# One kernel, four edits: values of the 16 context rows computed in front, u of two chunks in the stage before, 16-bit rounding and a rebuilt loop in the 8-bit feed forward, one block moved in the time mixing

## The chip, the core and the metric

The kernel runs on one core of a Trainium2 chip. The core has TensorE (PE; its weight loads, PEld, are shown apart), VectorE (DVE), ScalarE (ACT), GpSimd (POOL) and SyncE (SP, which here issues DMAs). The metric is the time of one execution on the device in microseconds, the median of several runs.

## The reference, cut to what matters

Four layers of three sublayers each work on x of 32 batches, 64 tokens and 256 features, and on a context of 32 x 128 rows of 128 features. Each sublayer computes `x = x + f(layernorm(x))`. These are the ones that the change touches.

The narrow cross attention (layers 1 to 3) splits the 128 context rows of a batch: the last 16 ("dca") have keys and values from weights of their own.

```python
kv_dca = (y_dca @ Wkv_dca + bkv_dca).reshape(b, DCA, 2, H, HD)
k_dca = _ln(kv_dca[:, :, 0], kn_dca_w, kn_dca_b);  v_dca = kv_dca[:, :, 1]
q = _ln((x @ Wq + bq).reshape(b, s1, H, HD), qn_w, qn_b)
...
ctx = _attn(qT, k, v) + DCA_WEIGHT * _attn(qT, k_dca, v_dca)   # two softmaxes
return ctx @ Wo + bo
```

The feed forward of layer 2 rounds the operands of its products to 8-bit floats and keeps results in bf16:

```python
def _qdot(x, w, out_dtype=BF16):
    return jnp.dot(x.astype(E4M3), w.astype(E4M3), preferred_element_type=out_dtype)
gate_value = jax.nn.gelu(_qdot(x, w_gating[0]))
activations = gate_value * _qdot(x, w_gating[1])
return _qdot(activations, w_linear)
```

The state space layer of layer 3 runs `h = exp(delta * A) * h + delta * B_t * xc` over the 64 tokens for 512 channels and 16 states, and sums `h * C_t` over the states. The product `delta * xc` is called u. The time mixing of layer 2 is a WKV recurrence with exponents, and a sigmoid gate r.

## The kernel before, in words

The twelve sublayers are blocks that follow one another (`SUBLAYERS`, L3680). In a block each engine has its own list of instructions, in the order in which the code issues them; counters (`sem[...]`) tell one engine what another has done, and nothing else sets the order. Activations lie transposed: features on the 128 partitions, the 2048 tokens as columns in four chunks of 512 (`CH`).

**Narrow cross attention (function from L1380).** In front of the loop the norm, the merged weights and the first three units of queries and keys are made. `widen(2)` (L1563) is the last of these, with a `keep_warm` (L79) on each side; `keep_warm` multiplies ones into a bank that nobody reads. Then come 36 steps. In step n TensorE makes the scores of batch n+1 (L1576) in the four banks `p_s`, the values of batch n-2 (L1587), the mixture of batch n-3 (L1615), turns the probabilities of batch n-2 (L1602), and every second step makes an output product (L1622). The units left over are spread over the steps: products (L1537, L1541), variance (L1553), widening (L1563). The values product has 512 columns: the first 256 by the main weights, the last 256 by the dca weights, of which only 16 rows are used. ScalarE copies both parts into `vx` (L1741, and L1743 for the 16 rows). VectorE takes the maxima of the scores (L1803), subtracts (L1813), sums (L1821), inverts (L1824), multiplies a unit (L1797) and adds the output (L1829). GpSimd scales the probabilities (L1889).

**Time mixing.** ScalarE's list begins with the norm, keys and values of chunk 0, then `gate(0)` (a load of the sigmoid table, two sigmoids L2736, a load of the exponential table) and then `exponents(0, 0)` and `exponents(0, 1)` (L2750, L2756).

**8-bit feed forward (`gated_fp8`).** 16 pairs of hidden tiles, each 2 x 128 features by 512 tokens. For a pair TensorE makes gate and up of two tiles (L2979, eight products) and adds the pair before the last but one to the output (`down`, L2993, four products; `LAG` is 2). ScalarE copies gate and up to bf16 (L3035, L3036), takes the gelu (L3038), and unloads an output chunk (L3019). VectorE's `round_pair` multiplies (L3064), cuts out the exponent (L3066), makes from it a large number (L3071), and adds and subtracts it (L3073, L3077), which rounds to 8-bit precision. The sum between the two, `moved`, is an f32 tile. VectorE also rounds the inputs in chunks (`move_h`, L3049 to L3057), scales the norm of the last two chunks and adds the residual (L3081). ScalarE's inverse of that norm (L3026 to L3029) lies behind the fourth pair.

**State space (`state_space`).** A first block makes `xc`, `delta` and the rows of B and C. The main block goes over 8 chunks of 256 columns and 16 states. ScalarE makes decay factors (L3540), GpSimd or TensorE the driving term, VectorE scans (L3607, L3609), GpSimd or VectorE weighs, TensorE sums (L3487). For the states 1, 4, 7, 10 and 14 the driving term comes from TensorE (L3471) by a turned copy of u (L3461, copied at L3524) and diagonals of B (L3517). GpSimd makes u of a chunk in `begin` (L3557) and marks batch starts (L3561): of chunk 0 at the block's start, of the next chunk at state 7. TensorE begins with eight warming products, two turns, and four warming products.

## Time and profile before

| | us |
|---|---|
| three runs | 2979.25, 2980.6, 2981.99 (median 2980.6) |
| profiled execution, device time | 2980.97 |
| its span | 2979.2 |
| TensorE busy | 2686.3 (90%) |
| VectorE busy | 1851.0 (62%) |
| ScalarE busy | 1409.8 (47%) |
| GpSimd busy | 1041.1 (35%) |
| mean granted TensorE clock | 0.971 of full speed |

The shares are averages over stages with different limits, so they are to be read stage by stage. By the first and last instruction of each, the narrow attentions run from 850.4 to 1058.0, from 1499.4 to 1708.7 and from 1945.5 to 2153.2; the time mixing from 1708.7 to 1844.5, the 8-bit feed forward to 1945.5, the state space layer's first block from 2153.2 to 2277.3 and its main block to 2685.7. An f32 product of TensorE stands in the trace as two records. A granted clock of 1.0 is 2.4 GHz and 0.5 is 1.2 GHz.

### The profile page before, as it was taken

How to read it: one execution, taken by the hardware profiler on the slowest of the kernel's cores; microseconds unless marked ns; L12 is line 12 of the kernel's file. 1: busy time of each engine (PE TensorE's matmuls, PEld its weight loads, DVE VectorE, ACT ScalarE, POOL GpSimd, SP SyncE). 2: the span in 40 equal slices, each digit the busy share in tenths (PEclk: the TensorE clock that was granted, in tenths of full speed). 3: DMA queues.
4: the chain of work that ended last, by engine and by line, in shares of the span. 5: the costliest groups of instructions: out<-in, count | busy, mean ns of one | idle time of the engine just before them, and what ended most of it. 6: DMA issues, size and time to landing. Idle time of an engine off the chain costs nothing. (4 is left out here: it accounts for less than half of the span.)

```text
span 2979.2 us, 51028 instructions
## 1 busy us (share of the span) xinstructions
PE 2686.3 (90%) x19340; PEld 1704.2 (57%) x19344; DVE 1851.0 (62%) x2513; ACT 1409.8 (47%) x2684; POOL 1041.1 (35%) x885
## 2 busy tenths in 40 slices
PE   7999997999989998899989977689997889997998
PEld 5999963466656647533346623246643555554787
DVE  3666646322248827543558788968755999996332
ACT  3323335121147747432247775657676666652223
POOL 1222210133216614100026500035502999981562
PEclk9999999999999999999999988899999999999999
DMA  4000002311120000110000000000001111103224
GB/s 162 22 25 25 18 7 99 134 47 46 54 62 2 2 23 3 42 47 0 1 24 2 16 1 1 0 24 2 27 19 50 71 73 71 73 36 123 70 82 147
DMA packets 77017, 128.95 MB, mean 43 GB/s; under 512 B 12112, under 2 KB 54736, under 8 KB 76304
## 3 DMA queue, kind: packets, MB, share of 16 engines
q1 hardware_dynamic: 67888, 101.78, 10.2%
q0 software_dynamic: 8928, 24.39, 2.6%
q8 instruction: 138, 2.26, 0.3%
q14 instruction: 63, 0.52, 0.1%
HBM read 107.40 MB, written 18.74 MB: 42 GB/s over the span
## 5 line engine op out<-in xcount | busy, mean ns | idle before, releaser
L3577 POOL TENSOR_TENSOR h<-ssm_u,ss_bc 128x1024 f32<-128x1024 f32 x88 | 205.6, 2357 | 0.0
L3540 ACT ACTIVATE ssm_p_h<-ss_delta,ss_decay 128x256 f32<-128x256 f32 x352 | 146.5, 464 | 123.9 <-DVE ctxT L3614 81.7
L3487 PE MATMUL ssm_p_y<-ctxT,ident 128*128 128x512 f32 x412 | 187.7, 596 | 0.0
L684 POOL TENSOR_TENSOR xw_prob<-xw_prob,xw_rsum 128x512 f32<-128x512 f32 x64 | 65.2, 1040 | 259.2 <-DVE xw_rsum L633 259.2
L3609 DVE TENSOR_TENSOR_SCAN ssm_p_h<-ssm_p_h,h 128x1024 f32<-128x1024 f32 x64 | 145.8, 2279 | 8.9 <-ACT ssm_p_h L3540 6.8
L3567 POOL TENSOR_TENSOR ctxT<-ctxT,ss_bc 128x1024 f32<-128x1024 f32 x50 | 117.4, 2356 | 19.8 <-DVE ctxT L3607 19.8
L3487 PEld LDWEIGHTS ssm_p_y<-ctxT,ident 128*128 128x128 f32 x412 | 76.5, 192 | 79.2 <-issue 78.5
L515 PE MATMUL xw_p_q<-h,xw_m_h 128*128 (+1 forms) x1024 | 119.0, 277 | 1.3 <-PEq L61 1.3
L515 PEld LDWEIGHTS xw_p_q<-h,xw_m_h 128*128 128x128 f32 x1024 | 116.0, 192 | 7.0 <-issue 7.0
L3471 PE MATMUL ssm_p_h<-ssm_b_diagonal,ssm_uT 128*128 128x128 f32 x640 | 82.0, 282 | 41.7 <-DVE ctxT L3614 21.2
L523 PE MATMUL xw_p_q<-xw_u,xw_vo_h 128*128 128x128 f32 x1024 | 117.1, 275 | 1.2 <-ACT xw_u L587 1.2
L617 DVE TENSOR_TENSOR xw_prob<-xw_p_s,xw_mask_bias 128x512 f32<-128x512 f32 x64 | 43.5, 680 | 119.0 <-PE xw_p_s L534 112.0
L523 PEld LDWEIGHTS xw_p_q<-xw_u,xw_vo_h 128*128 128x128 f32 x1024 | 115.6, 192 | 1.6 <-ACT xw_u L587 1.6
L3471 PEld LDWEIGHTS ssm_p_h<-ssm_b_diagonal,ssm_uT 128*128 128x128 f32 x640 | 77.0, 195 | 65.5 <-issue 56.7
L2524 ACT ACTIVATE lmm_hidden<-lmm_p_h,vecs 128x512 f32<-128x512 f32 x64 | 43.8, 687 | 135.8 <-PE lmm_p_h L2462 120.2
L1232 DVE TENSOR_TENSOR L0f_hidden<-L0f_silu,L0b_p_u 128x512 f32<-128x512 f32 x39 | 26.8, 688 | 125.4 <-PE L0b_p_u L1167 109.6
L582 ACT ACTIVATE xw_prob<-xw_prob 128x512 f32<-128x512 f32 x64 | 38.9, 633 | 111.2 <-DVE xw_prob L624 111.2
L1141 POOL DMA_INDIRECT L0f_rows_out<-L0b_y,L0f_row_of x39 | 38.5, 986 | 146.7 <-DVE L0b_y L1240 146.7
L1889 POOL TENSOR_TENSOR L1x_prob<-L1x_prob,L1x_rsum 128x896 f32<-128x896 f32 x64 | 65.3, 1042 | 64.6 <-DVE L1x_rsum L1824 64.6
L1889 POOL TENSOR_TENSOR L3x_prob<-L3x_prob,L3x_rsum 128x896 f32<-128x896 f32 x64 | 65.3, 1042 | 64.3 <-DVE L3x_rsum L1824 64.3
L1889 POOL TENSOR_TENSOR L2x_prob<-L2x_prob,L2x_rsum 128x896 f32<-128x896 f32 x64 | 65.3, 1042 | 64.2 <-DVE L2x_rsum L1824 64.2
L1861 POOL MEMSET L2x_vx<- 128x1024 f32 x1 | 1.0, 956 | 244.7 <-POOLq L61 244.7
(872 smaller groups left out, 7104.6 us busy)
## 6 DMA issues: line engine op xcount, KB each, us to landing
ss_bc<-ss_bc_rows SPq DMA_DIRECT2D x24, 896.0 KB, 4.3
xw_ctx_rows<-in_ctx_rows SPq DMA_DIRECT2D x32, 256.0 KB, 2.6
ss_bc<-ss_bc_rows SPq DMA_DIRECT2D x8, 768.0 KB, 4.0
L3f_rows<-L3f_rows_out SPq DMA_DIRECT2D x16, 384.0 KB, 3.9
L0f_wg<-in_L_ffn_gate SPq DMA_DIRECT2D x9, 512.0 KB, 9.4
L0f_wu<-in_L_ffn_up SPq DMA_DIRECT2D x9, 512.0 KB, 9.5
L0f_wd<-in_L_ffn_down SPq DMA_DIRECT2D x9, 512.0 KB, 9.6
L0f_rows<-L0f_rows_out SPq DMA_DIRECT2D x16, 256.0 KB, 4.3
```

What stands on the lines that cost most here:

```text
L515: mm = pe.matmul(p_q5[:, q % 2, h % 4 // 2, :, h % 2, :], m_h[:, h, a, :], k.h[:, a, ts(i, P)], start=h % 4 == 0 and a == 0, stop=a == H2 ...
L523: mm = pe.matmul(p_q[:, 1, ts(o, P)], vo_h[:, h, ts(o, P)], us[:, h, :], start=h == 0 and o == 0, stop=h == NH - 1, skip_group_check=True)
L617: v.tensor_tensor(prob[:, b, part, :], p_s[:, part, :], bcast(bias[:, ts(n, S2)], 1, 4), ALU.add).then_inc(sem["masked_scores"], 1)
L684: g.tensor_tensor(prob[:, n % 2, part, :], prob[:, n % 2, part, :], bcast(rsum[:, 1, part], 2, S2), ALU.mult).then_inc(sem["normed"], 1)
L1889: scaled = g.tensor_tensor(prob[:, m % 4, :, :, s0:s1], prob[:, m % 4, :, :, s0:s1], bcast(rsum[:, 1, m % 4, seg, :, :], 3, s1 - s0), ALU. ...
L2524: act.activation(hh[:, slot, j, :], p_h[:, slot, :], ACT.Gelu_apprx_tanh, bias=bias1[:, m:m + 1]).then_inc(sem["gelued"], 1)
L3471: mm = pe.matmul(p_h[:, n % 2, e * CT + b * P:e * CT + b * P + P], uT[:, c % 2, b, ts(e, P)], db[:, i, b, :], start=True, stop=True, skip_ ...
L3487: mm = pe.matmul(p_y[:, 2 * half:2 * half + 2, :].rearrange("p e t -> p (e t)"), k.ident[:, :], weighed[n % RING_W][:, ts(half, CH)], star ...
L3540: i = act.activation(out[:, ts(e, CT)], delta[:, e, ts(c, CT)], ACT.Exp, scale=decay[:, E4 * s + e:E4 * s + e + 1])
L3567: g.tensor_tensor(tiles(weighed[n % RING_W]), tiles(weighed[n % RING_W]), bcast(bcs[:, row_c(s), :], 1, E4), ALU.mult).then_inc(sem["weigh ...
L3577: g.tensor_tensor(tiles(drive[n % RING]), u[:, c % 2, :, :], bcast(bcs[:, row_b(s), :], 1, E4), ALU.mult).then_inc(sem["driven_g"], 1)
L3609: v.tensor_tensor_scan(slot, factor, term, 0.0, ALU.mult, ALU.add).then_inc(sem["scanned"], 1)
```

## The change

**Attention.** The 16 dca rows of all batches are gathered at the start by GpSimd into the tile of `us`. After `widen(2)`, in place of the second `keep_warm`, TensorE makes the values of eight batches at a time in four products of 256 columns, in the banks `p_s` that the first scores need next. ScalarE copies them out in two copies, SP moves the 16 rows of each batch to partitions 0 to 15 with 32 DMAs, and ScalarE's second copy of a batch reads that tile. The values product in the loop has 256 columns. **Time mixing.** `gate(0)` stands behind `exponents(0, 0)`. **Feed forward.** `moved` is bf16, with a smaller large number. ScalarE copies gate and up of a tile in one instruction and takes the gelu of a pair in one; the inverse of the norm is behind the first copies; `LAG` is 3; the output tile has two buffers; VectorE's extra work is spread differently. **State space.** GpSimd makes u of chunks 0 and 1, and marks their starts, in the first block. The warming goes down to one product between the two turns; ScalarE makes diagonals one state at a time.

```diff
+            for n in range(B):
+                g, j = n // GROUP, n % GROUP
+                if j == 0:
+                    sp.wait_ge(sem["dca_copied"], g // 2 + 1)
+                    if g >= 2:
+                        sp.wait_ge(sem["v_copied"], GROUP * (g - 1))
+                sp.dma_start(dca_values[:, n % (2 * GROUP), :], dca_made[DCA * j:DCA * j + DCA, g, :]).then_inc(s_d[g], 16)
...
                     pe.wait_ge(sem["scaled"], EARLY)
+                    pe.wait_ge(sem["dca_copied"], B // GROUP // 2)
...
+            def values_of_dca():
+                pe.wait_ge(s_o, 32)
+                pe.wait_ge(sem["dca_gathered"], 1)
+                pe.wait_ge(sem["scaled"], 2)
+                for g in range(B // GROUP):
+                    mm = pe.matmul(p_sf[:, g // 2, ts(g % 2, D)], dca_keys[:, ts(g, P)], wv[:, 1, :], start=True, stop=True, skip_group_check=True)
+                    if g % 2 == 1:
+                        mm.then_inc(sem["dca_made"], 1)
...
-                pe.matmul(p_v[:, :], k.ctxT[:, ts(n, S2)], wv[:, :, :].rearrange("p n f -> p (n f)"), start=True, stop=True, skip_group_check=True).then_inc(sem["valued"], 1)
+                pe.matmul(p_v[:, 0:D], k.ctxT[:, ts(n, S2)], wv[:, 0, :], start=True, stop=True, skip_group_check=True).then_inc(sem["valued"], 1)
...
             widen(2)
-            keep_warm(pe, k, p_tw[:, 0, :], 1)
+            values_of_dca()
...
-                    act.copy(own(m, slice(0, DCA)), p_v[0:DCA, D:2 * D].rearrange("p (g j d) -> p g j d", j=2, d=HD)).then_inc(sem["v_copied"], 1)
+                    if m % GROUP == 0:
+                        act.wait_ge(s_d[m // GROUP], 16 * GROUP)
+                    act.copy(own(m, slice(0, DCA)), dca_values[:, m % (2 * GROUP), :].rearrange("p (g j d) -> p g j d", j=2, d=HD)).then_inc(sem["v_copied"], 1)
...
+            for n in range(B // GROUP // 2):
+                act.wait_ge(sem["dca_made"], n + 1)
+                act.copy(dca_made[:, 2 * n:2 * n + 2, :].rearrange("p g f -> p (g f)"), p_sf[:, n, :]).then_inc(sem["dca_copied"], 1)
...
+            g.tensor_copy(dca_keys.rearrange("p (b s) -> p b s", s=DCA), k.ctxT[:, :].rearrange("p (b s) -> p b s", s=S2)[:, :, 0:DCA]).then_inc(sem["dca_gathered"], 1)
...
             keep(0, 1)
-            gate(0)
+
...
             exponents(0, 0)
+            gate(0)
             exponents(0, 1)
...
-    NP, LAG = PAIRS * NCH, 2
+    NP, LAG = PAIRS * NCH, 3
...
-        gb = sb(k, ctx, "gate", [P, 2, CH], BF16)
-        ub = sb(k, ctx, "up", [P, 2, 2, CH], BF16)
+        gu = sb(k, ctx, "gate_up", [P, 2, 2, 2, CH], BF16)
...
-        mv = sb(k, ctx, "moved", [P, 2, CH])
+        mv = sb(k, ctx, "moved", [P, 2, CH], BF16)
         aq = sb(k, ctx, "act", [P, LAG + 1, 2, CH], BF16)
-        yb = sb(k, ctx, "out", [P, H2, CH], BF16)
+        yb = sb(k, ctx, "out", [P, 2, H2, CH], BF16)
...
-                    pe.wait_ge(sem["copied"], 2 * (m - 1))
+                    pe.wait_ge(sem["copied"], m - 1)
...
-                if 1 <= n < 3:
-                    ln.var(pe, n - 1)
                 if n >= LAG:
                     down(n - LAG)
                 if n < NP:
                     project(2 * n + 1)
+                if n == 0:
+                    ln.var(pe, 0)
+                    ln.var(pe, 1)
...
-            act.preload_act_table(ACT.Gelu_apprx_tanh)
...
-                if c >= 1:
-                    act.wait_ge(sem["residual"], c)
-                act.copy(yb[:, :, :], outs[c % 2][:, :, :]).then_inc(sem["unloaded"], 1)
+                if c >= 2:
+                    act.wait_ge(sem["residual"], c - 1)
+                act.copy(yb[:, c % 2, :, :], outs[c % 2][:, :, :]).then_inc(sem["unloaded"], 1)
+
+            for n in range(NP):
+                if n > LAG + 1 and (n - LAG - 2) % PAIRS == PAIRS - 1:
                     unload((n - LAG - 2) // PAIRS)
-                if m == 8:
-                    act.preload_act_table_set("natural_log_exp_and_others")
+                if n >= 2:
+                    act.wait_ge(sem["product"], n - 1)
+                for j in range(2):
+                    act.wait_ge(sem["proj"], 2 * n + j + 1)
+                    act.copy(gu[:, n % 2, j, :, :], p_g[:, j, :, :]).then_inc(sem["copied"], 1)
+                if n == 0:
                     ln.inverse(act, 0)
                     ln.inverse(act, 1)
                     act.preload_act_table(ACT.Gelu_apprx_tanh)
-                act.wait_ge(sem["proj"], m + 1)
-                if n >= 2:
-                    act.wait_ge(sem["product"], n - 1)
-                if m >= 2:
-                    act.wait_ge(sem["gelued"], m - 1)
-                act.copy(gb[:, m % 2, :], p_g[:, m % 2, 0, :]).then_inc(sem["copied"], 1)
-                act.copy(ub[:, n % 2, m % 2, :], p_g[:, m % 2, 1, :]).then_inc(sem["copied"], 1)
-                act.wait_ge(sem["copied"], 2 * m + 1)
-                act.activation(ge[:, n % 2, m % 2, :], gb[:, m % 2, :], ACT.Gelu_apprx_tanh).then_inc(sem["gelued"], 1)
-            unload(NCH - 1)
+                act.wait_ge(sem["copied"], 2 * n + 2)
+                act.activation(ge[:, n % 2, :, :], gu[:, n % 2, :, 0, :], ACT.Gelu_apprx_tanh).then_inc(sem["gelued"], 1)
+            for c in range((NP - LAG - 2) // PAIRS, NCH):
+                unload(c)
...
-                v.tensor_scalar(mg[:, :, :], ex[:, :, :], FP8_MIN_NORMAL, FP8_MAGIC, ALU.max, ALU.mult).then_inc(sem["magic"], 1)
+                v.tensor_scalar(mg[:, :, :], ex[:, :, :], FP8_MIN_NORMAL, FP8_MAGIC16, ALU.max, ALU.mult).then_inc(sem["magic"], 1)
                 v.wait_ge(sem["magic"], n + 1)
                 v.tensor_tensor(mv[:, :, :], ac[:, :, :], mg[:, :, :], ALU.add).then_inc(sem["moved"], 1)
...
-                if n == 4:
-                    ln.scale(v, 0)
-                    ln.scale(v, 1)
-                elif n in (5, 6):
-                    move_h(n - 3)
+                if n in (3, 7):
+                    ln.scale(v, n // 4)
+                elif n in (4, 8):
+                    move_h(n // 4 + 1)
...
+                g.wait_ge(sem["delta"], 1)
+                g.wait_ge(sem["xc"], E4)
+                for c in range(MADE):
+                    make_input(g, c).then_inc(sem["input"], 1)
+                g.wait_ge(sem["input"], MADE)
+                for c in range(MADE):
+                    mark_starts(g, c)
...
-            keep_warm(pe, k, p_t[:, :], 8)
             turn(0, 0)
+            keep_warm(pe, k, p_o[:, :, :].rearrange("p o t -> p (o t)"), 1)
             turn(0, 1)
-            keep_warm(pe, k, p_o[:, :, :].rearrange("p o t -> p (o t)"), 4)
             driven(1)
...
-            for i in range(NT_):
-                for b in range(2):
-                    diagonal(0, i, b)
+            for b in range(2):
+                diagonal(0, 0, b)
             for n in range(TOTAL):
                 c, s = n // N, n % N
-                act.wait_ge(sem["starts"], c + 1)
+                if c >= MADE:
+                    act.wait_ge(sem["starts"], c + 1 - MADE)
...
-                if n < 2:
-                    turned(0, n)
+                if n == 0:
+                    turned(0, 0)
+                    turned(0, 1)
+                if 1 <= n < NT_:
+                    for b in range(2):
+                        diagonal(0, n, b)
...
-                if c >= 2:
-                    g.wait_ge(sem["turned"], 2 * (c - 1))
-                g.tensor_tensor(u[:, c % 2, :, :], delta[:, :, ts(c, CT)], xc[:, :, ts(c, CT)], ALU.mult).then_inc(sem["input"], 1)
-                g.wait_ge(sem["input"], c + 1)
-
-                first = delta[:, :, ts(c, CT)].rearrange("p e (b t) -> p e b t", t=S)[:, :, :, 0:1]
-                g.tensor_scalar(first, first, 0.0, 1e28, ALU.mult, ALU.add).then_inc(sem["starts"], 1)
+                g.wait_ge(sem["turned"], 2 * (c - 1))
+                make_input(g, c).then_inc(sem["input"], 1)
+                g.wait_ge(sem["input"], c + 1 - MADE)
+                mark_starts(g, c).then_inc(sem["starts"], 1)
...
-            begin(0)
```

TensorE in front of the third attention's loop, before (`L3x_p_t`: the warming's bank, `L3x_p_s`: the scores' banks, `L3x_rv`: inverse deviations):

```order
L1553 MATMUL L3x_p_y<-L3x_square,L3x_tally 32x128 x8
L79 MATMUL L3x_p_t<-ones 128x512
L1563 MATMUL L3x_p_s<-L3x_rv,L3x_heads 128x128 x8
L79 MATMUL L3x_p_t<-ones 128x512
L1576 MATMUL L3x_p_s<-L3x_k,L3x_qx 128x128 x8
```

and now (`L3x_u` holds the gathered dca rows, `L3x_wv` the value weights):

```order
L1566 MATMUL L3x_p_y<-L3x_square,L3x_tally 32x128 x8
L80 MATMUL L3x_p_t<-ones 128x512
L1576 MATMUL L3x_p_s<-L3x_rv,L3x_heads 128x128 x8
L1599 MATMUL L3x_p_s<-L3x_wv,L3x_u 128x256 x4
L1590 MATMUL L3x_p_s<-L3x_k,L3x_qx 128x128 x8
```

The warming product between widening and scores has become four products into the banks that the scores take next.

ScalarE in the feed forward, from the table load to the first gelus, before:

```order
L3011 ACT_TABLE_LOAD
L208 ACTIVATE f_ln_square<-h 128x1024 x2
L3014 ACT_TABLE_LOAD
L3035 CAST f_gate<-f_p_g 128x512
L3036 CAST f_up<-f_p_g 128x512
L3038 ACTIVATE f_gelu<-f_gate 128x512
```

and now (`f_gate_up` holds both halves of a pair):

```order
L3041 ACT_TABLE_LOAD
L209 ACTIVATE f_ln_square<-h 128x1024 x2
L3057 CAST f_gate_up<-f_p_g 128x1024 x2
L215 ACTIVATE f_ln_rstd<-f_ln,eps 128x512
L217 ACTIVATE f_ln_rstd<-f_ln_rstd 128x512
L215 ACTIVATE f_ln_rstd<-f_ln,eps 128x512
L217 ACTIVATE f_ln_rstd<-f_ln_rstd 128x512
L3061 ACT_TABLE_LOAD
L3063 ACTIVATE f_gelu<-f_gate_up 128x1024
L3057 CAST f_gate_up<-f_p_g 128x1024 x2
```

The inverse of the norm (L214, L216, now L215, L217) has moved from behind the fourth pair to ahead of the first gelu, and one table load has gone from the start.

TensorE at the start of the state space layer's main block, before (`ssm_p_t`: turned u, `ssm_b_diagonal`: diagonals of B):

```order
L79 MATMUL ssm_p_t<-ones 128x512 x8
L3461 MATMUL ssm_p_t<-ident,ssm_u 128x128 x8
L79 MATMUL ssm_p_o<-ones 128x512 x4
L3471 MATMUL ssm_p_h<-ssm_b_diagonal,ssm_uT 128x128 x16
L3481 MATMUL ssm_p_y<-ss_xc,ss_diag 128x256 x4
```

and now:

```order
L3503 MATMUL ssm_p_t<-ident,ss_u 128x128 x4
L80 MATMUL ssm_p_o<-ones 128x512
L3503 MATMUL ssm_p_t<-ident,ss_u 128x128 x4
L3513 MATMUL ssm_p_h<-ssm_b_diagonal,ssm_uT 128x128 x16
L3523 MATMUL ssm_p_y<-ss_xc,ss_diag 128x256 x4
```

The turns stand first, and of twelve warming products one is left, between them.

## Rows read from the trace of the kernel before

**Rows 1.** busy time by stage; columns as in its first line
```profile
core 0: us, PE busy (x) PEld busy (x) DVE busy (x) ACT busy (x) POOL busy (x), PEclk, DMA share, GB/s
...
1844.50:1945.50 101.00, 66.67 (x208) 25.10 (x212) 87.39 (x104) 63.22 (x110) 0.00 (x0) 0.81 0.00 1
1945.50:2153.20 207.70, 192.13 (x2548) 125.64 (x2548) 159.34 (x266) 139.65 (x288) 108.14 (x119) 0.99 0.03 10
...
2277.30:2685.70 408.40, 363.01 (x1432) 217.62 (x1433) 374.83 (x208) 244.65 (x610) 372.70 (x169) 0.99 0.17 61
```

**Rows 2.** timeline of TensorE, one batch of the third narrow attention
```profile
2090.06 0.73 PE L1576 MATMUL L3x_p_s<-L3x_k,L3x_qx 32*128 32x128 f32 x16
2090.71 1.12 PE L1587 MATMUL L3x_p_v<-L3x_wv,ctxT 128*128 128x512 f32 x2
2093.38 0.65 PE L1553 MATMUL L3x_p_v<-L3x_square,L3x_tally 128*32 128x128 f32 x16
```

**Rows 3.** groups by line: the values product, and one of 256 columns
```profile
L1587 PE MATMUL L3x_p_v<-L3x_wv,ctxT 128*128 128x512 f32 x64 | 35.3, 633 | 0.0
L3452 PE MATMUL ssm_p_o<-ss_z,ss_w_out 128*128 128x256 f32 x128 | 29.0, 380 | 1.3 <-DVE ss_z L3588 1.3
```

**Rows 4.** waits of VectorE in that attention's loop (1979 to 2140)
```profile
DVE L3x_nmax L1803 <- PE L3x_p_s L1576: 10.2, 14, 2.7
DVE x L1829 <- PE L3x_p_y L1622: 6.2, 7, 2.5
```

**Rows 5.** timeline of VectorE, two batches near the loop's end
```profile
2124.53 1.28 DVE L1803 TENSOR_REDUCE L3x_nmax<-L3x_p_s 128x8 f32<-128x896 f32 x2
2132.73 1.27 DVE L1803 TENSOR_REDUCE L3x_nmax<-L3x_p_s 128x8 f32<-128x896 f32 x2
```

**Rows 6.** timeline in front of the loop: warming and first scores
```profile
1977.48 1.13 PE L79 MATMUL L3x_p_t<-ones 128*128 128x512 f32 x2
1978.97 0.73 PE L1576 MATMUL L3x_p_s<-L3x_k,L3x_qx 32*128 32x128 f32 x16 [0.36 <-DVE L3x_k L1797]
```

**Rows 7.** groups by line in the 8-bit feed forward
```profile
L3064 DVE TENSOR_TENSOR f_product<-f_gelu,f_up 128x1024 bf16<-128x1024 bf16 x16 | 11.0, 687 | 7.7 <-ACT f_gelu L3038 7.5
L3071 DVE TENSOR_SCALAR f_magic<-f_exponent 128x1024 bf16<-128x1024 bf16 x16 | 6.8, 427 | 0.6
L3073 DVE TENSOR_TENSOR f_moved<-f_product,f_magic 128x1024 f32<-128x1024 bf16 x16 | 19.6, 1226 | 0.6
L3019 ACT CAST f_out<-f_p_y 128x1024 bf16<-128x1024 f32 x2 | 2.0, 1012 | 0.0
```

**Rows 8.** timeline there: ScalarE's table loads, VectorE's products
```profile
1852.28 1.28 ACT L3014 ACT_TABLE_LOAD   x1
1853.57 0.58 ACT L3035 CAST f_gate<-f_p_g 128x512 bf16<-128x512 f32 x1
1856.69 0.69 DVE L3064 TENSOR_TENSOR f_product<-f_gelu,f_up 128x1024 bf16<-128x1024 bf16 x1 [1.68 <-ACT f_gelu L3038]
1877.82 0.69 DVE L3064 TENSOR_TENSOR f_product<-f_gelu,f_up 128x1024 bf16<-128x1024 bf16 x1 [3.58 <-ACT f_gelu L3038]
```

**Rows 9.** timeline of ScalarE, first sigmoid block of the time mixing
```profile
1736.61 0.60 ACT L2736 ACTIVATE tm_gate<-tm_p_p 128x512 f32<-128x512 f32 x1 [0.94 <-PE tm_p_p L2648]
```

**Rows 10.** timeline, start of the state space main loop
```profile
2277.36 9.24 PE L79 MATMUL ssm_p_t<-ones 128*128 128x512 f32 x16 [7.74 <-PEq L61]
2291.70 1.95 PE L3471 MATMUL ssm_p_h<-ssm_b_diagonal,ssm_uT 128*128 128x128 f32 x16
2293.75 2.29 DVE L3607 TENSOR_TENSOR_SCAN ctxT<-h,ssm_p_h 128x1024 f32<-128x1024 f32 x1 [6.96 <-PE ssm_p_h L3471]
2298.37 3.43 PE L3471 MATMUL ssm_p_h<-ssm_b_diagonal,ssm_uT 128*128 128x128 f32 x16 [4.72 <-DVE ctxT L3607]
```

**Rows 11.** timeline there, GpSimd's second u and a wait behind it
```profile
2307.69 2.36 POOL L3557 TENSOR_TENSOR ssm_u<-ss_delta,ss_xc 128x1024 f32<-128x1024 f32 x1
2322.04 2.30 DVE L3609 TENSOR_TENSOR_SCAN ssm_p_h<-ssm_p_h,h 128x1024 f32<-128x1024 f32 x1 [0.93 <-POOL h L3577]
```

36 lines of the change are left out of this document (23 added, 13 removed).

## The prediction

> **What bounds the kernel now.** I read the busy time by stage first, because one core runs twelve sublayers behind one another and the change touches six of them: three narrow cross attentions, the time mixing, the 8-bit feed forward and the state space layer. In each I then read who waits, and last the timeline at the edited place. The reader is to see three different bounds. In the cross attention (207.7 us, the other two within 2 us of it) TensorE is busy for 192.1 us and VectorE for 159.3 [rows 1], and VectorE's waits in the loop over batches are for scores and output products of TensorE [rows 4]. In the feed forward VectorE is busy for 87.4 of 101.0 us, and in the main loop of the state space layer for 374.8 of 408.4, with GpSimd at 372.7 [rows 1]. So TensorE's time counts in the attentions, VectorE's in the feed forward, and in the state space layer what delays the first scans.
>
> **Attention, loop: -7.5 us a layer.** The values product of a batch goes from 512 to 256 columns. It is two records per product, 64 in a layer [rows 3], 1.12 us of TensorE with no idle time around them [rows 2]. A record of 512 columns lasts 592 ns where nothing delays it and one of 256 lasts 380 on average [rows 3], so a record loses 0.213 us, a batch 0.427 and the layer 13.6. That is the most that it can give, and VectorE's waits in the loop, 10.2 and 6.2 us [rows 4], leave room for it. It is not all got: VectorE waits for scores 14 times in 32 batches, and each wait gives back at most what TensorE has saved since the one before, and never more than its own length. Where VectorE does not wait, the batch is set by its own work: maximum, subtraction, sum and reciprocal, 4.1 us (two batches from 2124.53 to 2132.73 [rows 5]), against 3.3 of TensorE from a batch's scores to the next part in one without a projection (2090.06 to 2093.38 [rows 2]). The last eight batches and some in the middle are such. That leaves 16 to 20 batches of 0.427: 6.8 to 8.5, and I take 7.5. Bounds: 4 (every second wait is replaced by one for GpSimd or ScalarE) and 11. The second copy per batch stays on ScalarE, now from the SBUF tile; ScalarE has idle time of its own before these copies, so its source costs nothing that shows. The 32 DMAs of 16 KB wait on SP only for the copies and are wanted over 15 us later.
>
> **Attention, front: +1.2 us a layer.** A warming product (two records, 1.13 us) goes; four products of 256 columns, eight records, come, and two copies of 512 columns on ScalarE. Before, the last widening is issued by 1977.48, where the warming begins, and the scores start at 1978.97, released by VectorE's multiplication [rows 6]. Now the records take 8 x 0.227 = 1.8 us (29.0 us for 128 records [rows 3]), the first copy lies beside the second half, and the second copy (about 0.6, half of the 1.01 of a copy of 1024 [rows 7]) stands behind the last record with two hand-overs of some 0.15: 1980.2. The multiplication is hidden now, the copy is what is late. Bounds 0.5 and 2.5. The gather on GpSimd stands at the stage's start, where it has nothing else to do. Three layers: 3 x (-7.5 + 1.2) = -19.
>
> **Time mixing: -1 us.** ScalarE's first sigmoid block waits 0.94 us for TensorE in its middle [rows 9]; now the first exponents stand ahead of it and the product is there when it is reached. Both table loads stay. What is queued behind is the same. Bounds 0 and -3.
>
> **Feed forward: -19 us.** Per pair VectorE does 0.687 + 2 x 0.427 + 2 x 1.226 us [rows 7]; the exponent's operation (L3066) is as long as that of L3071, the subtraction (L3077) as long as the addition. The two last write or read an f32 tile; with that tile 16 bit wide they have the types of the product row, 0.687. So 1.08 us a pair, 16 pairs, -17.2. Then the waits: VectorE waits 7.7 us for gelus [rows 7], 3.58 of it behind ScalarE's block of two table loads and four activations [rows 8]. The block moves ahead of the first gelu and one pair of loads is gone. ScalarE: two copies (0.9 each as issued one behind the other) from 1852.3, the four activations 2.6, a load 1.28, a gelu of 1024 about 1.0 (as the copy of 1024): the first product starts at 1859.1 and not 1856.7, +2.4. The other waits (0.9 + 0.2 + 3.6 + 1.2) go, -5.9. ScalarE then needs 2 x 0.9 + 1.0 = 2.8 us a pair, VectorE 2.9, plus 0.9 a pair for h, the norm and the residual. TensorE's twelve records a pair are 2.6 us at the full clock and 5.2 at half, and the granted clock of the stage is 0.81 [rows 1]. It has an idle stretch of some 3 us behind its first two pairs, as before, and I expect the next records at 1.2 GHz while VectorE has nothing in reserve: +1.7. Sum -17.2 - 5.9 + 2.4 + 1.7 = -19. What is late next is ScalarE in the pairs without other work on VectorE. Bounds: -10 (half clock in half of the pairs) and -22.
> What the Trainium skill adds here (ScalarE: Activation LUTs, "What ACT_TABLE_LOAD costs") is that a switch of tables costs a drain of about 1.4 us beside the 1.28. The trace disagrees: the load at 1852.28 lasts 1.28 and the work behind it starts at 1853.57 [rows 8]. By the page's rule the stage would gain 1.4 more.
>
> **State space: -9 us.** Before, TensorE warms for 9.24 us ahead of the two turns of u and 3.6 behind them, so that the products of state 1 start at 2291.7 and VectorE's second scan at 2293.75 after 6.96 us of idle [rows 10]. Now u is there when the block opens at 2277.3: first turn beside ScalarE's table load (1.28), two diagonals 0.6, decay factors 1.7 (2280.8), copy 0.6, second turn 1.1, copy 0.6, so 2283.2. The products take 1.95 us, or 3.43 as the next ones do at half clock [rows 10]; with the warming gone I take 3.4. Second scan at 2286.7: -7. GpSimd's 2.36 us of u for the second chunk at 2307.7 go from the first chunk too; VectorE's two waits on GpSimd behind it, 0.93 and about 1.2, go: -2 [rows 11]. The rest of the layer is VectorE and GpSimd in step and shifts as it is. In the stage before, GpSimd does both chunks of u with nothing else to do. Bounds -5 (further products at half clock) and -12.
>
> **Sum.** -19 - 1 - 19 - 9 = -48 us on a profiled span of 2979.2; that execution took 2980.97, 0.4 above the median 2980.6. The prediction is 2933 us.
>
> **Rivals.**
> A. VectorE takes over in the attentions. For it: in the tail of the loop it is the bound already, and its busy time is 159 us of 208. Against: TensorE is at 192, and 16 us of waits on it are real [rows 4]. Then the loop gives 2 a layer and the front costs 1.2: total -48 + 16.5 = -31, 2949 us.
> B. The feed forward changes its bound to TensorE. For it: twelve records at half clock (5.2 us) are longer than the new VectorE pair. Against: with a shorter pair TensorE rests less than it did in the pairs that ran at full clock. Price: half of 16 pairs at 5.2 in place of 3.8, +9 to +11: 2943 us.
> C. The 16-bit add and subtract run at the f32 rate, so that this part does not do what it says. The product row with the same three types speaks against it. Then the feed forward gains waits alone, -2: 2950 us.
> D. Slower than before: TensorE doesn't come up to 2.4 GHz in the state space layer. Its full-clock records there were preceded by sixteen dense warming records; now there are two, and turns. In a chunk TensorE works about 46 of 51 us at full clock; at half it would need some 35 more. It decides the sign from one and a half chunks on: with two at 1.2 GHz the time is 2933 + 70 = 3003 us. Against: at 2298 half clock was granted and left again within the next few groups, while the work was the same as now.
> What the Trainium skill says (TensorE: Matmul & The Clock Gate, on the transpose mode) is that transposes don't count as activity; by it the turns in front do not help to raise the clock. No row here separates turns from other work. It would favour D, or the half clock that I have assumed for the first products.
> E. More than forecast: all waits fall together with less half clock (loop 11 a layer, feed forward -22, state space -12): 2917 us.
>
> **How the numbers follow.** Forecast 0.62, A 0.14, B 0.10, C 0.03, D 0.02, E 0.09. The range reaches from near E to A's time: 2919 to 2949. About 0.2% (6 us) is what a measurement of this kernel can tell from no change. All cases but D are more than 29 us faster; for unseen couplings between the four edits I leave a little more: faster 0.95, same 0.02, slower 0.03.
>
> **What would show it.** In the profile after: values records near 380 ns with 13 us less of TensorE in each attention and fewer waits of VectorE for scores; scores starting about 1.2 us later behind the widening; f_moved and f_act at 0.69 us, no wait of VectorE over 2 us behind its first product, stage near 82 us; the second scan 9 to 10 us behind the block's start where it was 16.4. It is wrong if VectorE's waits in the attentions come back under another releaser, if TensorE's granted clock in the feed forward falls below 0.8, or if the first chunk of the state space layer stays at 1.2 GHz.

## The result: 45 us faster, 2 us from the forecast

The changed kernel takes 2934.8 us (median of four runs, 2928.7 to 2940.7), the kernel before on the same chip 2979.9 (2974.8 to 2982.0): a ratio of 0.985, 95% interval 0.983 to 0.987. The forecast was 2933. The profiled execution of the changed kernel is the slowest of its four (span 2938.9), so the two traces differ by 40.3 us, not by 45.

Where these 40.3 us are, measured from a stage's first instruction to the next stage's first:

| stage | before | after | difference | forecast |
|---|---|---|---|---|
| narrow attentions, 1st, 2nd, 3rd | 207.9, 209.3, 207.7 | 202.6, 203.4, 203.9 | -5.3, -5.9, -3.8 | -6.3 each |
| time mixing | 135.8 | 134.6 | -1.2 | -1 |
| 8-bit feed forward | 101.0 | 80.0 | -21.0 | -19 |
| projections of the state space layer | 124.1 | 128.2 | +4.1 | 0 |
| its main loop | 408.4 | 400.4 | -8.0 | -9 |
| all other stages | | | +0.8 | 0 |

The busy times by stage in the profile after (third attention, feed forward, projections, main loop), to be laid beside [rows 1]:
```profile
core 0: us, PE busy (x) PEld busy (x) DVE busy (x) ACT busy (x) POOL busy (x), PEclk, DMA share, GB/s
...
1911.70:2115.60 203.90, 183.37 (x2554) 129.02 (x2554) 158.26 (x266) 141.39 (x290) 108.79 (x120) 0.97 0.05 13
...
1831.70:1911.70 80.00, 60.30 (x208) 23.48 (x212) 69.88 (x104) 57.63 (x60) 0.00 (x0) 0.89 0.00 1
2115.60:2243.80 128.20, 110.30 (x356) 47.80 (x357) 65.45 (x78) 86.97 (x123) 7.44 (x9) 0.93 0.14 47
2243.80:2644.20 400.40, 355.45 (x1410) 215.28 (x1410) 374.64 (x208) 245.22 (x609) 367.80 (x164) 0.97 0.17 63
```
In the feed forward VectorE lost 17.5 us of work and the stage 21.0. In the third attention TensorE lost 8.8 us of busy time, front and half clock included, and the stage only 3.8, so more than half of what TensorE gave up there did not reach the end. The main loop of the state space layer kept its VectorE time, 374.8 and 374.6: what went is waiting.

**Feed forward.** The groups that answer to [rows 7], after:
```profile
L3099 DVE TENSOR_TENSOR f_moved<-f_product,f_magic 128x1024 bf16<-128x1024 bf16 x16 | 11.1, 693 | 0.6
L3103 DVE TENSOR_TENSOR f_act<-f_moved,f_magic 128x1024 bf16<-128x1024 bf16 x16 | 11.1, 691 | 0.5
L3090 DVE TENSOR_TENSOR f_product<-f_gelu,f_gate_up 128x1024 bf16<-128x1024 bf16 x16 | 11.0, 685 | 4.0 <-ACT f_gelu L3063 4.0
```
The add and the subtraction are at 0.69 us, as the forecast took from the product row. The 4.0 us of waiting are all ahead of the first product. Its place in the timeline, beside [rows 8]:
```profile
1843.74 1.28 ACT L3061 ACT_TABLE_LOAD   x1
1845.03 1.06 ACT L3063 ACTIVATE f_gelu<-f_gate_up 128x1024 bf16<-128x1024 bf16 x1
...
1846.20 0.69 DVE L3090 TENSOR_TENSOR f_product<-f_gelu,f_gate_up 128x1024 bf16<-128x1024 bf16 x1 [4.02 <-ACT f_gelu L3063]
```
The stage begins at 1831.7, so the first product comes 14.5 us in, where it came at 12.2: +2.3, forecast +2.4. From there to the end it takes 65.5 us instead of 88.8.

**Attention.** The third one's values product, beside [rows 3]:
```profile
L1610 PE MATMUL L3x_p_v<-L3x_wv,ctxT 128*128 128x256 f32 x64 | 21.8, 422 | 0.0
```
64 records fell from 35.3 to 21.8 us, 13.5, as worked out. VectorE's waits in the loop, beside [rows 4], in the waits of VectorE (total, times, longest):
```profile
DVE L3x_nmax L1831 <- PE L3x_p_s L1590: 10.8, 13, 2.7
DVE x L1857 <- PE L3x_p_y L1645: 4.2, 6, 2.1
```
The waits for scores stayed (14 of 10.2 us before), those for output products went from 6.2 to 4.2 us. From the first scores to the last the loop went from 156.8 to 150.4 us in the first layer, 156.4 to 151.3 in the second and 156.5 to 151.6 in the third. The front, beside [rows 6]:
```profile
1943.71 1.99 PE L1599 MATMUL L3x_p_s<-L3x_wv,L3x_u 128*128 128x256 f32 x8
1946.47 0.73 PE L1590 MATMUL L3x_p_s<-L3x_k,L3x_qx 32*128 32x128 f32 x16 [0.77 <-ACT L3x_dca_made L1814]
```
The scores start 34.8 us into the stage instead of 33.5 and are released by the second copy, as forecast: +1.3, and +1.5 in the first layer. In the second layer they start 0.5 us earlier than before (34.8 us in, before 35.2), but that is not the edit's: in the seven other profiles with the narrow product the second layer's front is 36.4 us, +1.2.

**State space layer.** Start of the main loop, TensorE and VectorE, beside [rows 10]:
```profile
2249.68 3.78 PE L3513 MATMUL ssm_p_h<-ssm_b_diagonal,ssm_uT 128*128 128x128 f32 x16 [0.68 <-ACT ssm_uT L3565]
...
2253.57 2.29 DVE L3648 TENSOR_TENSOR_SCAN ctxT<-h,ssm_p_h 128x1024 f32<-128x1024 f32 x1 [2.66 <-PE ssm_p_h L3513]
...
2268.62 1.95 PE L3513 MATMUL ssm_p_h<-ssm_b_diagonal,ssm_uT 128*128 128x128 f32 x16
```
The block opens at 2243.8: the second scan is 9.8 us behind it where it was 16.4. The first products run at 1.2 GHz (3.78 us against 1.95), the next ones too, and by 2268.6 the clock is up.

### The profile page after: what moved, and what is told of

Read it like the earlier page. It is cut to its first block and busy times, and to the rows that moved or that the text cites. A ratio compares the mean times of both kernels' runs of the same rounds, so it can differ in the third digit from the quotient of the medians.

```text
span 2938.9 us, 51051 instructions
## 1 busy us (share of the span) xinstructions
PE 2643.2 (90%) x19336; PEld 1706.3 (58%) x19340; DVE 1830.5 (62%) x2513; ACT 1411.4 (48%) x2640; POOL 1044.0 (36%) x888
## 5 line engine op out<-in xcount | busy, mean ns | idle before, releaser
L3618 POOL TENSOR_TENSOR h<-ss_u,ss_bc 128x1024 f32<-128x1024 f32 x88 | 205.7, 2358 | 67.5 <-POOLq L62 67.5
```

The source lines that it names most:

```text
L3618: g.tensor_tensor(tiles(drive[n % RING]), u[:, c % 2, :, :], bcast(bcs[:, row_b(s), :], 1, E4), ALU.mult).then_inc(sem["driven_g"], 1)
```

## Experiments: each part alone

All runs below share a chip with a kernel before of their own, 2968.5, 2975.7 or 2968.6 us, so that ratios, and within one chip times, are compared.

**Attention alone** (of the diff shown ahead, the hunks of the narrow cross attention).

> The kernel before with the attention part alone. Theory (TensorE binds only a part of the batches, the rest are VectorE's): each of the three narrow attentions is shorter by 4 to 6 us, -12 to -18 in all, 2962 to 2969 us, and the gain is a sum of steps between 0 and 0.43 us, with no gain in the last eight batches. Rival 1 (TensorE's time counts everywhere, 13.6 us a layer less the front): -37, 2943 us. Rival 2 (what is saved in one layer is given back behind it, since a TensorE that rests more starts the next stage at the lower clock): the attentions are as short as by the theory, but the state space layer's projections, which this kernel does not touch, take 4 us longer, as in the changed kernel; total -10.

2954.4 us beside 2968.5; ratio 0.996 (0.995 to 0.997). The attentions take 5.7, 4.0 and 5.6 us less than in the kernel before: the theory's size. All of TensorE's saving, rival 1, would have been 37. The projections of the state space layer took 126.6 us, which looks like rival 2; the table under the last group of runs comes back to it.

**Feed forward alone** (the hunks of `gated_fp8` and its constant).

> The kernel before with the 8-bit feed forward alone changed. Theory: the stage is bound by VectorE and goes from 101 to 80 us, 2960 us. Rival (the stage was short in the changed kernel only because TensorE's clock there, 0.90 as granted, was better than before, 0.82, by chance or by what the time mixing did): 83 to 85 us, 2964.

2948.7; ratio 0.993 (0.992 to 0.995). The stage is 80.1 us: the theory to 0.1. The gain needs neither of the other parts.

**State space part alone** (the hunks behind them).

> The kernel before with the state space part alone (u in front, less warming). Theory: the second scan 9 to 10 us behind the start of the main block where it was 16.4, the main block 7 to 9 us shorter, 2972 to 2973 us, and the projections ahead of it unchanged at 124 us, since the two products on GpSimd stand beside nothing. Rival (the products on GpSimd, and not the clock, made the projections 4 us longer in the changed kernel): projections at 128 us, total only -4.

2959.9; ratio 0.9975 (0.9966 to 0.9984). Second scan at 9.8 us, main loop 7.9 us shorter, projections 124.1 as before. So GpSimd's two products in the projections cost nothing, and the 4.1 us that appeared there in the changed kernel are not theirs.

The three ratios multiply to 0.987, the whole change has 0.985 (0.983 to 0.987): within the noise the parts do not disturb each other. The block moved in the time mixing has no run alone. A sum over whole programs is no finer than some us: the stages ahead of the first attention, which no edit touches, take 845.6 to 850.9 us in the 14 profiles. So the parts are better compared stage by stage. Inside the feed forward the parts do not simply add up.

**Rounding alone**, in the old loop:
```diff
-        mv = sb(k, ctx, "moved", [P, 2, CH])
+        mv = sb(k, ctx, "moved", [P, 2, CH], BF16)
...
-                v.tensor_scalar(mg[:, :, :], ex[:, :, :], FP8_MIN_NORMAL, FP8_MAGIC, ALU.max, ALU.mult)
+                v.tensor_scalar(mg[:, :, :], ex[:, :, :], FP8_MIN_NORMAL, FP8_MAGIC16, ALU.max, ALU.mult)
```

> The kernel before, and in the feed forward only the moved values in 16 bits with the smaller constant; its loop stays (two narrow copies and a gelu per block, the tables changed in the middle). Theory: VectorE saves 16 x 1.08 = 17.2 us, but ScalarE, at 2 x (0.59 + 0.60 + 0.65) = 3.7 us a pair and 68 us with its other work behind the first product, takes over: the stage loses 15 to 18 of the 17.2 + 5.9, 83 to 86 us, 2962 to 2966, and VectorE's waits for gelus grow. Rival (the two savings don't meet: the waits stay as long as they were, 7.7 us): exactly -17.2, with the waits at the same places. Rival 2 (the add and the subtraction run no faster on 16 bits in this loop): no change.

2957.7; ratio 0.997 (0.9955 to 0.998). The stage is 90.3 us, -10.7: less than the theory's 15 to 18. Two groups of VectorE in this kernel:
```profile
L3074 DVE TENSOR_TENSOR f_moved<-f_product,f_magic 128x1024 bf16<-128x1024 bf16 x16 | 11.1, 693 | 0.6
...
L3065 DVE TENSOR_TENSOR f_product<-f_gelu,f_up 128x1024 bf16<-128x1024 bf16 x16 | 11.0, 689 | 13.6 <-ACT f_gelu L3039 13.6
```
17.1 us of work went and the waits for gelus rose from 7.7 to 13.6. The direction is the theory's; its size was not, since I had still counted the old waits among the savings.

**Rebuilt loop alone**: the feed forward's hunks without those two lines:
```diff
         mv = sb(k, ctx, "moved", [P, 2, CH])
...
+        gu = sb(k, ctx, "gate_up", [P, 2, 2, 2, CH], BF16)
...
+                    act.copy(gu[:, n % 2, j, :, :], p_g[:, j, :, :]).then_inc(sem["copied"], 1)
```

> The kernel before, and in the feed forward only the rebuilt loop (joined copies, one gelu a pair, the norm's block ahead of the first gelu, one more pair of lag); the moved values stay 32 bits wide with the old constant. The rounding alone gave 10.7 us and VectorE's waits for gelus grew from 7.7 to 13.6 us. Theory (two bounds one behind the other, so that the edits are worth more together): VectorE has no wait for a gelu any more, and with the 17.2 us of wide rounding still there the stage is 80.0 + 17.2 = 97 us, -4 against before; 10.7 and 4 are 15 of the 21 that both give together. Rival (the parts add up): the loop alone gives the missing 10 us, stage 91 us.

2973.8 beside 2975.7; ratio 0.999 (0.998 to 1.0002), which by itself is no change. The stage is 97.1 us, the 97 expected:
```profile
L3070 DVE TENSOR_TENSOR f_moved<-f_product,f_magic 128x1024 f32<-128x1024 bf16 x16 | 19.6, 1226 | 0.6
...
L3061 DVE TENSOR_TENSOR f_product<-f_gelu,f_gate_up 128x1024 bf16<-128x1024 bf16 x16 | 11.0, 685 | 4.0 <-ACT f_gelu L3034 4.0
```
The old waits are gone, but that was 5.9 us for +2.3 at the front. Alone the edits give 10.7 and 3.9, together 21.0: the loop is worth 3.9 while VectorE is slow and 10.3 once it is fast, and what it then removes are the waits for gelus, 13.6 us in the old loop and 4.0 in the new one, all ahead of the first product.

## Experiments: the start of the state space layer

**Less warming alone**, u still made in the main loop:
```diff
-            keep_warm(pe, k, p_t[:, :], 8)
             turn(0, 0)
+            keep_warm(pe, k, p_o[:, :, :].rearrange("p o t -> p (o t)"), 1)
             turn(0, 1)
-            keep_warm(pe, k, p_o[:, :, :].rearrange("p o t -> p (o t)"), 4)
```

> The kernel before, and in the state space layer only the warming products cut from eight ahead and four behind the turns to one between them; u is still made by GpSimd in the main block. Theory: u costs GpSimd 2.36 us, and ScalarE's ten diagonals and its wait for the starts then delay the copies, so that the second scan comes 12 to 13 us behind the block's start (16.4 before, 9.8 with both edits): main block 3 to 5 us shorter of the 7.9 that both give. Rival 1 (the warming was the whole delay): 7 to 8 us. Rival 2 (the warming carried the clock through the first chunk): the products stay at 1.2 GHz for a chunk and the block is longer than before.

2972.3 beside 2975.7; ratio 0.9988 (0.998 to 0.9997). Second scan 12.4 us in, main loop 4.0 us shorter: the theory. Its VectorE row (the block starts at 2275.25):
```profile
2287.63 2.29 DVE L3606 TENSOR_TENSOR_SCAN ctxT<-h,ssm_p_h 128x1024 f32<-128x1024 f32 x1 [2.94 <-PE ssm_p_h L3471]
```

**The old warming in the changed kernel**, u in front:
```diff
+            keep_warm(pe, k, p_t[:, :], 8)
             turn(0, 0)
-            keep_warm(pe, k, p_o[:, :, :].rearrange("p o t -> p (o t)"), 1)
             turn(0, 1)
+            keep_warm(pe, k, p_o[:, :, :].rearrange("p o t -> p (o t)"), 4)
```

> The changed kernel with the old warming put back (eight ahead of the turns of u, four behind). Theory: u in front is then worth nothing for the start, since the warming covers GpSimd's work as it did before: second scan 16.4 us behind the block's start, and of the 7.9 us only the relief of GpSimd in the first chunk stays, 1 to 2 us; main block 410 us where it is 403.7, total +6 to +7 against the changed kernel. Rival (the products at full clock behind the warming give back what the warming takes): no difference to the changed kernel.

2939.0 on a chip whose kernel before takes 2975.7; ratio 0.988 (0.986 to 0.990). Main loop 406.6 us against 400.4 in the changed kernel and 408.4 before: +6.2. (The expectation's measure of 403.7 reaches 3.3 us into the next stage; by it this kernel takes 409.8, the 410 expected.) Against the changed kernel the ratios' intervals overlap, so this rests on the stage's own time. The start, TensorE's timeline and then VectorE's (the block starts at 2241.55):
```profile
2241.59 8.89 PE L80 MATMUL ssm_p_t<-ones 128*128 128x512 f32 x16 [7.75 <-PEq L62]
...
2255.52 1.95 PE L3513 MATMUL ssm_p_h<-ssm_b_diagonal,ssm_uT 128*128 128x128 f32 x16
2262.19 3.65 PE L3513 MATMUL ssm_p_h<-ssm_b_diagonal,ssm_uT 128*128 128x128 f32 x16 [4.72 <-ACT ssm_b_diagonal L3559]
```
```profile
2257.57 2.29 DVE L3649 TENSOR_TENSOR_SCAN ctxT<-h,ssm_p_h 128x1024 f32<-128x1024 f32 x1 [8.89 <-PE ssm_p_h L3513]
```
12.5 us of warming bought one group at 1.95 us instead of 3.78, and the next, behind an idle stretch of 4.72, was at 1.2 GHz again. u in front is worth nearly nothing for the start as long as the warming covers GpSimd (second scan 16.0 us in, before 16.4; the loop is 1.8 us shorter); less warming alone is worth 4.0 of the 7.9.

## Experiments: what binds the attentions now

TensorE gave up 13.5 us a layer and the loop 5 to 6. Three kernels take more from one engine each, in all three layers of the changed kernel.

**TensorE: 16 columns of the values product.**
```diff
-                pe.matmul(p_v[:, 0:D], k.ctxT[:, ts(n, S2)], wv[:, 0, :], start=True, stop=True, skip_group_check=True)
+                pe.matmul(p_v[:, 0:16], k.ctxT[:, ts(n, S2)], wv[:, 0, 0:16], start=True, stop=True, skip_group_check=True)
```

> The changed kernel, and in the three narrow attentions each batch's values product computes 16 of its 256 columns; the other columns of the values are left out. It takes another 0.5 to 0.6 us of TensorE from each batch, after the 0.427 of the change. Theory (after the change TensorE binds in 10 to 12 of 32 batches, and VectorE's own work in the others): the steps of 5.74, 6.33, 4.84 and 7.22 us shorten until VectorE or ScalarE binds, the others not: -3 to -5 us a layer, -9 to -15 in all. Rival 1 (TensorE's time is worth the same share as in the change, 5.2 of 13.6): -7 a layer, -20 in all. Rival 2 (VectorE already binds everywhere): nothing.

**VectorE: half of each sum.**
```diff
-                        total = v.tensor_reduce(rsum[:, 0, m % 4, seg, :, :], prob[:, m % 4, :, :, s0:s1], AX, ALU.add)
+                        total = v.tensor_reduce(rsum[:, 0, m % 4, seg, :, :], prob[:, m % 4, :, :, s0:s0 + (s1 - s0) // 2], AX, ALU.add)
```

> The changed kernel, and in the three narrow attentions VectorE sums only half of each row of exponents (the other half of the sum is left out). That takes about 0.5 us of VectorE from each batch, 16 a layer. Taking another 0.2 us a batch from TensorE gave nothing in the loop (151.6 us from the first scores to the last, as before it). Theory (VectorE is the bound after the change): the tail of the loop, seven steps of 3.6 to 4.3 us, shortens by 0.4 to 0.5 each, the steps of 3.55 to 5.6 too, 5 to 10 us a layer, -15 to -30 in all. Rival (GpSimd's normalisation, or the chain through all engines, is the bound): the tail alone shortens or nothing does, under -3 a layer.

**GpSimd: half of each row normalised.**
```diff
-                        scaled = g.tensor_tensor(prob[:, m % 4, :, :, s0:s1], prob[:, m % 4, :, :, s0:s1], bcast(rsum[:, 1, m % 4, seg, :, :], 3, s1 - s0), ALU.mult)
+                        scaled = g.tensor_tensor(prob[:, m % 4, :, :, s0:s0 + (s1 - s0) // 2], prob[:, m % 4, :, :, s0:s0 + (s1 - s0) // 2], bcast(rsum[:, 1, m % 4, seg, :, :], 3, (s1 - s0) // 2), ALU.mult)
```

> The changed kernel, and in the three narrow attentions GpSimd multiplies only half of each row by the reciprocal (the other half stays without it). That takes about 1 us of GpSimd's 2.04 from each batch. Theory (VectorE is the bound): at most 1 us a layer, where TensorE's turns wait for GpSimd. Rival (the chain through GpSimd took over when TensorE was relieved): -3 to -8 us a layer, more than from VectorE's half sums.

Ratios to the kernel before: 0.985 (0.984 to 0.987), 0.981 (0.979 to 0.982) and 0.985 (0.984 to 0.987), where the changed kernel has 0.985. Only VectorE's gave something: 2911.5 us beside 2926.4 of GpSimd's on one chip, and against that kernel 5.4, 3.8 and 3.6 us in the three stages. In the first, 2.5 us are its loop's third step, 8.87 us there and 6.40 here, which moves with the granted clock. The busy times of the third layer's loop, one row from each of the three kernels (TensorE's, then VectorE's, then GpSimd's; columns as in the table of stages above):
```profile
1945.60:2097.20 151.60, 132.47 (x2104) 103.06 (x2105) 135.93 (x236) 111.69 (x233) 94.23 (x105) 0.95 0.02 6
```
```profile
1938.10:2087.00 148.90, 138.22 (x2104) 101.94 (x2105) 123.18 (x236) 111.72 (x233) 94.34 (x105) 0.97 0.02 6
```
```profile
1949.30:2100.80 151.50, 138.24 (x2104) 101.87 (x2105) 135.73 (x236) 112.18 (x233) 69.78 (x105) 0.97 0.02 6
```
The first took 5.8 us more from TensorE (138.3 in the changed kernel) and the loop stayed at 151.6: nothing, as rival 2 of that run had it, and not the theory. (Its reason, VectorE everywhere, is another matter; see below.) Some steps of the middle did shorten by 0.3 us, but the step behind each grew by as much. A record of 16 columns still lasts 269 ns, so it was 0.3 us a batch and not 0.5 to 0.6, and the granted clock of the loop fell to 0.95 (0.97 after the change, 0.99 before it), which shows in its steps at the loop's start. GpSimd lost 24.5 us and nothing moved. VectorE lost 12.7 us and the loop 2.7.

But the theory for VectorE, 5 to 10 us a layer, is wrong as well. The steps from scores to scores say where, in us (third layer; the steps behind batches 8 to 14, and the last five):

| kernel | batches 8 to 14 | last five |
|---|---|---|
| before | 6.75, 4.98, 4.56, 6.16, 3.90, 5.87, 5.27 | 3.55, 4.21, 3.99, 4.22, 3.98 |
| after | 6.33, 4.88, 4.56, 5.74, 3.55, 5.58, 4.84 | 3.62, 3.93, 4.27, 3.93, 4.27 |
| TensorE relieved | 6.02, 5.18, 4.56, 5.69, 3.55, 5.58, 4.54 | 3.62, 3.93, 4.27, 3.93, 4.27 |
| VectorE relieved | 6.33, 4.88, 4.55, 5.74, 3.55, 5.55, 4.84 | 3.55, 3.79, 3.55, 3.79, 3.55 |
| GpSimd relieved | 6.33, 4.87, 4.55, 5.74, 3.55, 5.58, 4.84 | 3.62, 3.93, 4.26, 3.93, 4.27 |

Of the 2.7 us that the relief of VectorE gave this loop 1.8 are in these last five steps, 0.5 in the third step of the loop and 0.3 in one of the middle. Elsewhere in the middle its idle time grew instead (batch 12: from 0.85 to 1.78 us). So VectorE sets the pace of the tail and hardly any of the rest. The step of 3.55 us did not move for any of the three. ScalarE's timeline through it, in the changed kernel, and through the same step of the kernel before:
```profile
2009.56 1.05 ACT L1755 ACTIVATE L3x_prob<-L3x_prob 128x1024 f32<-128x1024 f32 x1
...
2010.52 0.34 ACT L1764 COPY L3x_vx<-L3x_p_v 128x256 f32<-128x256 f32 x1
...
2010.90 0.41 ACT L1768 COPY L3x_vx<-L3x_dca_values 16x256 f32<-16x256 f32 x1
...
2011.21 0.25 ACT L1774 COPY L3x_u<-L3x_p_y 128x128 f32<-128x128 f32 x1
2011.50 1.07 ACT L1784 COPY L3x_probT<-L3x_p_t 128x512 f32<-128x512 f32 x2
```
```profile
2044.89 0.37 ACT L1741 COPY L3x_vx<-L3x_p_v 128x256 f32<-128x256 f32 x1 [0.43 <-PE L3x_p_v L1587]
...
2046.06 1.07 ACT L1759 COPY L3x_probT<-L3x_p_t 128x512 f32<-128x512 f32 x2 [0.25 <-PE L3x_p_t L1602]
```
Before, ScalarE waited 0.43 us there for the values product, which is what the change shortened by 0.43. After it no gap is left: the five groups, six operations, stand end to end. So in such steps it looks as if ScalarE took over after 0.34 of the 0.43 us. That ScalarE binds there is read from its timeline; no run relieved ScalarE itself. The other steps of the middle have no single engine without idle time all through, and I leave their bound at "a chain over engines".

## Experiments: two tries at a faster kernel

**Feed forward: the norm and h's rounding on GpSimd.**
```diff
+        @block.gpsimd
+        def _(g):
+            for c in range(DONE, NCH):
+                ln.scale(g, c - DONE)
+            for c in range(DONE, NCH):
+                move_h(g, c)
...
-                if n in (3, 7):
-                    ln.scale(v, n // 4)
-                elif n in (4, 8):
-                    move_h(n // 4 + 1)
+                if n in (2, 6):
+                    exponent(v, n // 4 + DONE)
```

> The changed kernel, and in the feed forward the norm's scaling and the rounding of h for the last two chunks (all but the exponent) are done by GpSimd, which had nothing to do there. Theory (VectorE is the bound, with ScalarE close behind it): VectorE is rid of 2 x (1.22 + 0.69 + 1.22 + 1.22) = 8.7 us, ScalarE with 3.0 us a pair takes over, and the stage goes from 80 to 73 or 75 us. Rival 1 (GpSimd beside VectorE slows VectorE's 16-bit work, as both share a path to memory): f_moved and f_act above 0.75 us, stage no shorter than 78. Rival 2 (ScalarE is the bound already): no change.

2927.1 us; ratio 0.986 (0.984 to 0.987): nothing. The stage is 80.1 us, although 8.7 us of work left VectorE. Its groups there:
```profile
L3102 DVE TENSOR_SCALAR f_exponent<-f_product 128x1024 int16<-128x1024 int16 x16 | 11.9, 745 | 0.6
...
L3109 DVE TENSOR_TENSOR f_moved<-f_product,f_magic 128x1024 bf16<-128x1024 bf16 x16 | 11.1, 692 | 0.6
...
L3107 DVE TENSOR_SCALAR f_magic<-f_exponent 128x1024 bf16<-128x1024 bf16 x16 | 10.4, 652 | 0.6
```
The outcome is rival 1's, but on other operations than I named: f_moved stays at 0.69, while the exponent and the magic, 0.43 us each before and after, now average 0.75 and 0.65. The timeline of both engines shows how:
```profile
1845.23 4.65 POOL L202 TENSOR_TENSOR h<-h,f_ln_rstd 128x1024 f32<-128x1024 f32 x2 [146.56 <-ACT f_ln_rstd L217]
...
1848.87 1.56 DVE L3100 TENSOR_TENSOR f_product<-f_gelu,f_gate_up 128x1024 bf16<-128x1024 bf16 x1 [4.02 <-ACT f_gelu L3063]
...
1859.46 4.01 POOL L3080 TENSOR_SCALAR f_h_magic<-f_h_exponent 128x1024 bf16<-128x1024 f32 x1 [9.57 <-DVE f_h_exponent L3072]
...
1860.00 1.14 DVE L3102 TENSOR_SCALAR f_exponent<-f_product 128x1024 int16<-128x1024 int16 x1
...
1861.63 0.69 DVE L3109 TENSOR_TENSOR f_moved<-f_product,f_magic 128x1024 bf16<-128x1024 bf16 x1
...
1863.55 2.13 POOL L3082 TENSOR_TENSOR f_h_moved<-h,f_h_magic 128x1024 f32<-128x1024 f32 x1
...
1863.69 2.27 DVE L3102 TENSOR_SCALAR f_exponent<-f_product 128x1024 int16<-128x1024 int16 x1
1865.75 2.18 POOL L3084 TENSOR_TENSOR f_h_rounded<-f_h_moved,f_h_magic 128x1024 bf16<-128x1024 f32 x1
1865.99 2.22 DVE L3107 TENSOR_SCALAR f_magic<-f_exponent 128x1024 bf16<-128x1024 bf16 x1
```
The last exponent and the last magic each ended 0.28 us behind the two-source instruction of GpSimd beside it, 2.27 and 2.22 us instead of 0.43, and the first product, 1.56 instead of 0.69, 0.55 behind one. Beside GpSimd's one-source instruction of 4.01 us one exponent took 1.14, but f_moved ran at its 0.69; no f_moved stood beside a two-source instruction, so how it would fare there this run does not show. The groups of exponent, magic and product grew by 5.1, 3.6 and 0.8 us, 9.5 together, and took back the 8.7.
The Trainium skill (GPSIMD Engine Reference, Specifications) says that GpSimd shares its interfaces to SBUF with VectorE and contends with instructions of VectorE in a two-port mode or with two SBUF inputs. The trace agrees for the product, which has two inputs in SBUF and stood still until GpSimd's two-source instruction was over. It does not agree for f_moved, which has two as well and lost nothing beside the one-source instruction. Whether the exponent and the magic run in a two-port mode no row shows.

**The same, with a warmer TensorE and one table load less.**
```diff
                 step(n)
+            pe.wait_ge(sem["shifted"], B)
+            keep_warm(pe, k, p_sf[:, 0, :], 1)
...
                 turn(NCH - 1)
+                pe.wait_ge(sem["ln_centred"], NCH)
+                keep_warm(pe, k, ln.p_mean[:, 0, :], 3)
...
-            act.preload_act_table_set("natural_log_exp_and_others")
-
             def diagonal(c, i, b):
```

> The changed kernel with the feed forward's edit of the run before and two more: the state space block keeps the table that the projections left (no load at its start) and TensorE runs six warming records behind the last projection, where it idled for 7.8 us; and two warming records stand behind the last output product of each narrow attention. Theory: feed forward -5 to -7; second scan of the state space layer at 5 to 7 us behind the block's start where it was 9.8 (1.3 from the table, up to 1.9 from products at full clock); the norm at the start of the projections at full clock, 592 ns a record, -4 where it was at 1061. In all -8 to -14 against the changed kernel. Rival (the clock does not follow such warming): the products of the first states stay at 3.7 us, and the projections stay between 122 and 128 us by chance: -6 to -8.

2918.1 us (2915.5 to 2924.0), ratio 0.984 (0.982 to 0.985): 9 us faster than the kernel without these edits on the same chip, 2927.1 (2924.8 to 2929.4). Not all of it is the edits': the two profiles lie 13.9 us apart, and 4.2 of these are ahead of the first attention, where both kernels are the same. The rest is mainly the time mixing, 3.4, the main loop, 3.0, and the stages between the first two narrow attentions, 2.9. Against the changed kernel itself, 0.985 (0.983 to 0.987) on another chip, the intervals overlap, so that comparison is not settled by itself. The main loop is 397.1 us where the changed kernel has 400.4. The block starts at 2232.8; TensorE's timeline and then VectorE's:
```profile
2237.44 2.05 PE L3527 MATMUL ssm_p_h<-ssm_b_diagonal,ssm_uT 128*128 128x128 f32 x16 [0.68 <-ACT ssm_uT L3577]
2244.21 3.45 PE L3527 MATMUL ssm_p_h<-ssm_b_diagonal,ssm_uT 128*128 128x128 f32 x16 [4.72 <-ACT ssm_b_diagonal L3570]
```
```profile
2239.60 2.29 DVE L3660 TENSOR_TENSOR_SCAN ctxT<-h,ssm_p_h 128x1024 f32<-128x1024 f32 x1 [0.73 <-PE ssm_p_h L3527]
```
Second scan 6.8 us in, within the 5 to 7 expected, with the first products at 2.05 us: warming in an idle stretch of the stage ahead gave the first products the full clock and delayed nothing, where warming at the start costs more than it gives. The next group, behind 4.72 us of idle time, was at 1.2 GHz again. The norm of the projections ran at 592 ns a record, as expected too, but the 4 us did not come: the stage took 126.1 us. One table over all profiles shows why (projections, in us; first its kernel):

| wide values product | narrow values product |
|---|---|
| before 124.1, feed forward alone 125.5, space alone 124.1, rounding alone 122.1, loop alone 125.5, warming alone 124.1 | changed 128.2, attention alone 126.6, old warming 122.2, TensorE relieved 120.7, half sums 122.2, half normalised 122.2, GpSimd 127.0, both 126.1 |

The stage takes 122 to 126 us with the wide product, 124.2 on average, and 121 to 128 with the narrow one, 124.4. What it takes goes with the clock granted over its first 121 us: 0.93 in the changed kernel (128.2 us), 0.94 with the attention alone and in the GpSimd kernel (126.6, 127.0), 0.96 with the feed forward alone (125.5), 0.98 in four kernels (122.1 and three times 122.2), 0.99 with TensorE relieved (120.7). The half clock falls in it at different places. In the changed kernel it covers the first 10 us (granted 0.52), behind 1.94 us in which TensorE was idle. With the feed forward alone it comes about 10 us later. Two rows of busy times of that kernel, and TensorE's timeline:
```profile
2131.40:2135.10 3.70, 3.69 (x8) 1.44 (x8) 1.33 (x2) 1.05 (x1) 0.00 (x0) 1.00 1.09 349
2137.90:2144.10 6.20, 6.19 (x8) 2.58 (x9) 0.93 (x2) 1.26 (x2) 0.00 (x0) 0.50 0.00 0
```
```profile
2137.91 10.18 PE L3206 MATMUL ssp_p_a<-h,ss_bc 128*128 128x512 f32 x16 [2.79 <-DVE h L202]
```
The clock was 1.0 up to an idle stretch of 2.79 us, and behind it 0.5 for 6.2 us of dense work. So the +4.1 is not a lasting cost of the change: two kernels with the same attention and feed forward have less than the kernel before (122.2, with the old warming and with GpSimd relieved). It is a spread of the clock from program to program that my sum did not carry. Rival 2 of the first run is refuted in its size, since the average does not rise. But a half clock right at the stage's start occurs in six of the eight kernels with the narrow product and in none of the six with the wide one, so where it falls does seem to depend on the attention ahead.

## Why the prediction was right, point by point

- **Bounds by stage.** Right for all three kinds of stage, and the stages share the gain accordingly: half of the gain comes from the stage where VectorE was the bound, a fifth from a shorter start of the state space loop, and TensorE's largest saving gave the least per microsecond.
- **Attention, loop: -7.5 a layer.** The mechanism was right and the size too large: -6.4, -5.1, -4.9, within the bounds of 4 and 11. The term that was mis-sized is "16 to 20 batches of 0.427". In the third layer seven steps gave 0.42 to 0.43, four 0.34, three 0.29 and one 0.10, 5.3 us in all; the rest none, and the third step of the loop moved with the clock (8.87 to 7.66 us in the first layer, 8.54 to 8.88 in the third). So the -6.4 of the first layer has 1.2 us of luck in it. The lower bound had named ScalarE as what could replace a wait, and that is what its timeline shows in the steps of 3.55. That VectorE's waits for scores would become clearly fewer was wrong: 14 waits of 10.2 us became 13 of 10.8.
- **Attention, front: +1.2.** +1.5 and +1.3 in the first and third layer, released by the second copy as the prediction put it; -0.5 in the second, which the seven other profiles (+1.2) do not repeat. The values records average 422 ns, not 380.
- **Time mixing: -1.** -1.2 in the two traces, but the seven profiles with the moved block average 135.5 us (133.0 to 136.6) and the seven without it 135.6. Nothing can be told from it: the -1 is within the spread, and no run shows that it is there.
- **Feed forward: -19.** -21.0. The 17.2 (17.1 of the rounding group), the waits and the +2.4 (measured +2.3) came as written, and the rounding alone and the loop alone bear the split out. The +1.7 for half clock did not come: the granted clock was 0.89, up from 0.81, and VectorE never waited behind its first product. In the old loop ScalarE came next (the rounding alone showed it); what comes next in the new one no run shows.
- **Rule of the Trainium skill there** (ScalarE: Activation LUTs, "What ACT_TABLE_LOAD costs"): the load at 1843.74 lasts 1.28 us and the gelu starts at 1845.03, so again no drain of 1.4 us shows. The stage went from four loads to two, so by that rule ScalarE would have been spared 2.8 us of drains and not the 1.4 that the prediction named.
- **State space layer: -9.** -8.0. Second scan 6.6 us earlier (7 forecast), products at 1.2 GHz as assumed (3.78 for 3.4), waits for GpSimd in the first chunk from 2.1 us to 0.6. The two runs on the warming gave each half its share.
- **Rule of the Trainium skill on transposes** (TensorE: Matmul & The Clock Gate, on the transpose mode): the products behind the turns were at 1.2 GHz in the changed kernel, but there was idle time as well, and no run here tells the two apart. The third state's products on TensorE ran at full clock in every run, and rival D has nothing for it.
- **Rivals.** A (VectorE takes over in the attentions, 2 a layer) is refuted: 5 to 6 came. B is refuted (clock 0.89). C is refuted by the row of f_moved. D and E did not happen.
- **Sum: right in the parts, lucky in the last figure.** The parts missed by +0.4 to +2.5 a layer in the attentions, -2 in the feed forward and +1 in the state space layer; +4.1 in untouched projections is the largest single error in the trace. The median of the four runs lies 6 us under the profiled one, so the forecast is closer to it, 2 us, than my sum is to the trace, 8 us. Being within 2 is luck; 8 is what the working was good for.

## What to carry to other kernels

Price a saving on an engine that is not alone in binding by steps, not by its total: list the time from one iteration to the next, and for each step ask which engine has no gap left; here 13.5 us of TensorE were worth 5. Two edits on producer and consumer of one loop are to be judged together, since the rebuilt loop was worth 3.9 us before the rounding and 10.3 behind it. Warm TensorE in an idle stretch ahead of a stage rather than at its start, and before handing work to GpSimd look at what VectorE runs beside it, since a short operation there can wait for the rest of GpSimd's instruction.

## What the runs showed of the hardware

- Five 16-bit operations of VectorE that met a two-source instruction of GpSimd ended only behind it: 2.22 to 2.27 us for operations of 0.43, 1.56 for one of 0.69. Beside a one-source instruction of GpSimd of 4.0 us f_moved kept its 0.69, and one exponent took 1.14.
- A product of 16 columns in f32 lasts 269 ns a record, one of 256 columns 422 in the same loop. Going from 512 columns to 256 took 211 ns off a record, going on to 16 only 153.
- TensorE's granted clock stayed at 0.5 through 6.2 us of dense work behind an idle stretch of 2.79 us. The same stage took 120.7 us where 0.99 of the clock was granted and 128.2 where it was 0.93, with the other 12 programs between them.
